# Sine attention with a mixture of experts on one core: the values of two units are summed together behind every fourth slot's scores

## Chip, core and metric

The kernel runs on one core of one Trainium2 chip. The metric is the device time of one execution in microseconds; the time before is 473.99, the median of three runs (473.74 to 475.28).

## What is computed

x has 8 rows of 512 tokens of 128 numbers. The reference, cut to what matters:

```python
# attention, 16 heads of 8, on the normalised x
logits = jnp.einsum('bhqd,bhkd->bhqk', Q, K) / scale
attn = jnp.sin(OMEGA_0 * logits)
out = jnp.einsum('bhqk,bhkd->bhqd', attn, V)
x = x + jnp.einsum('bsd,ed->bse', out, Wo) + bo
# experts, on the normalised x: one shared, eight routed of which each token takes two
out = shared                      # silu(x @ Wg.T) * (x @ Wu.T) @ Wd.T
for e in range(E_ROUTED):
    out = out + cw[..., e:e + 1] * _expert(x, Wg[e], Wu[e], Wd[e])
x = x + out
```

There is no softmax: a sine is taken of every score, and its products with V are summed over the keys.

## The kernel before, in words

Each engine has a program of its own, written out by hand over one common count of slots, `a`. A row of x has 32 slots (`SLOTS`); b is the row and s the slot in it. In slot s ScalarE takes one sine, of 128 keys x 512 queries x two heads (`sine`, line 888). Two slots make a unit: four heads and one tile of 128 keys, 16 units in a row (`UNITS`). Behind slot 256 (`TAIL`) there are no more sines, only the rest of the experts' tiles.

On TensorE, in every even slot s, stand the scores of slots s and s+1 (`scores`, line 638: two matmuls each, on 64 rows of the array each, that run together). They go to `score[0]` and `score[1]`, two banks of PSUM each; the scores of slot u wait until the sine of slot u-2 has read the same buffer (`sined`). Behind them stand the values of one earlier unit (`sum_values`, line 651: four heads of 32 columns side by side, each in fp32, eight matmul instructions in all), added into `o_ps` over the 16 units of a row. They read one of four buffers `attn` (`RING`); the sine of unit k waits until unit k-4 is summed (`summed`). The first unit of a row waits until `copy_o` (line 895 on ScalarE from row 3 on, line 1003 on VectorE in the rows before) has read `o_ps` of the row before, in slot 3.

Behind the values come, in this order: in odd slots from row 1 on, where the plan has a tile, `down` of an earlier tile (six matmuls, lines 778 to 780) and `gate_up` of a new one (twelve, lines 760 to 762); and the projections of the next row, the output projection, the transpose and the routing of the row before, each in a slot of its own (`S_Q` = 3: line 607; `S_K` = 8: line 614; `S_V` = 11: line 620; `S_OUT` = 6: line 664; `S_XT2` = 16: line 677; `S_ROUTE` = 19; `S_PREFIX` = 23). `gate_up` has one bank `g_ps` until slot 258, so it waits until `hid` of the tile before it (line 1220 on VectorE, behind ScalarE's silu, line 909) has read it; `down` comes six slots behind its tile.

ScalarE takes in every slot the sine, then the slot's silu, then the slot's copies (`copy_xt` line 869 in slot 2, `scale_q` 875 in slot 4, `scale_k` 881 in slot 9, `copy_o` in slot 3, `copy_x2` 899 in slot 17; in rows 0 to 2 VectorE has these copies). All waits are on semaphores, and an engine's instructions go in the order of its program.

The values of unit k stand in slot 2k + 4 (`LAG`); units 14 and 15 of a row stand in slots 0 and 2 of the next row (`LAST_SUMS`), those of the last row in slots 256 and 257 (`TAIL_SUMS`).

Of the kernel before, what the change touches and what calls it, by code (L numbers as in the profile page):

```python
# [16 lines left out]
ROWS, SEQ, DM = 8, 512, 128  # L17
# [41 lines left out]
SLOTS = 2 * GROUPS * TT  # L59
UNITS = SLOTS // 2  # L60
RING = 4
LAG = 4
LAST_SUMS = {0: 14, 2: 15}
TAIL = ROWS * SLOTS
TAIL_SUMS = {0: 14, 1: 15}

# [227 lines left out]
def sine_attention_moe_kernel(nc, x, wq, bq, wk, bk, wv, bv, wo, bo, wgu, wd, wr, rb, ident, out):  # L296
    with ExitStack() as ctx:
# [293 lines left out]
        def _(pe):  # L591
# [13 lines left out]
            def project_q(n, bank):  # L605
                pe.wait_ge(xt_ready, n + 1)
                pe.matmul(bank, wq_s[:, :], xn_t[:, :], start=True, stop=True).then_inc(q_done, 1)
# [16 lines left out]
            def scores(b, u):  # L624
                j, kt, h = u // 2 // TT, u // 2 % TT, u % 2
                if b == 0 and kt == 0:
                    pe.wait_ge(q_placed, 2 * j + h + 1)
                    pe.wait_ge(k_placed, 2 * j + h + 1)
                if b and u == 0:
                    pe.wait_ge(q_loaded, b * 64)  # L630
                    pe.wait_ge(k_loaded, b * 64)
                if b or u >= 2:
                    pe.wait_ge(sined, b * SLOTS + u - 1)
                elif u == 1:
                    pe.wait_ge(v_ready, 1)
                for i in range(2):
                    rows = slice(64 * i, 64 * i + 64)
                    mm = pe.matmul(score[h][:, i, :], keys[b % 2][rows, 2 * j + h, kt * P:(kt + 1) * P],  # L638
                                   queries[b % 2][rows, 2 * j + h, :], start=True, stop=True)
                mm.then_inc(scored, 1)  # L640

            def sum_values(b, k):
                j, kt = k // TT, k % TT
                pe.wait_ge(sined, b * SLOTS + 2 * k + 2)
                if k == 0:
                    pe.wait_ge(v_ready, b + 1)
                    if b:
                        pe.wait_ge(o_ready, b)
                for i in range(PER):
                    h = (j * PER + i) * 32  # L650
                    mm = pe.matmul(o_ps[32 * i:32 * i + 32, :], vals[b % 2][:, kt, h:h + 32], attn[k % RING][:, i, :],  # L651
                                   start=(k == 0), stop=(k == UNITS - 1))
                mm.then_inc(summed, 1)
# [57 lines left out]
            def look_up(g, first, end):  # L711

                pe.wait_ge(experts_ready, g + 1)
                _, found = nc.values_load_multi_w_load_instructions(
                    expert[g][0:1, first:end], engines=[mybir.EngineType.PE], min_val=0, max_val=(ROUTED - 1) * P,
                    skip_runtime_bounds_check_because="tile_experts clamps the table")
                for k, value in enumerate(found):
                    place_of[g, first + k] = value
# [18 lines left out]
            def gate_up(i):  # L737
                kind, row, t, e = TILES[i]
                if kind == SPARSE:
                    n = LOAD_OF[RANK[i]]  # L740
                    first = (RANK[i] - LOADS[n][0]) * P
                    pe.wait_ge(xt_loaded[n % XT], 16 * (n // XT + 1))
                    hi, lo = (xt[n % XT][:, half, first:first + P] for half in range(2))
                else:
                    pe.wait_ge(x2t_ready, row + 1)
                    hi, lo = (x2_t[row % TURNED][:, half * SEQ + t * P:half * SEQ + (t + 1) * P] for half in range(2))
                pe.wait_ge(w_split, 1 if kind == SHARED else EXP)

                if i >= GU_MAIN + BANKS - 1:
                    pe.wait_ge(hid_ready, i - BANKS + 1)  # L750
                elif i:
                    pe.wait_ge(hid_ready, min(i, GU_MAIN))
                bank = gu_bank(i)
                look_ahead(i, GU_PIECES)
                for c in range(2 * CH):
                    if c == 2:
                        look_ahead(i + 1, GU_PIECES)
                    here = bank[:, c * P:(c + 1) * P]
                    hi_part, lo_part = piece(i, w_hi[c]), piece(i, w_lo[c])
                    pe.matmul(here, hi_part, hi, start=True, stop=False)  # L760
                    pe.matmul(here, hi_part, lo, start=False, stop=False)  # L761
                    mm = pe.matmul(here, lo_part, hi, start=False, stop=True)  # L762
                mm.then_inc(gu_done, 1)

            def down(i):
                wait_lo(pe, i)
                if i >= D_MAIN + BANKS:
                    wait_read(pe, i - BANKS)
                elif i:
                    wait_read(pe, min(i, D_MAIN) - 1)  # L770
                here = d_bank(i)
                look_ahead(i, D_PIECES)
                for c in range(CH):
                    if c == 1:
                        look_ahead(i + 1, D_PIECES)
                    hi, lo = (half[i % HB][:, c * P:(c + 1) * P] for half in (hid_hi, hid_lo))
                    hi_part, lo_part = piece(i, w_hi[2 * CH + c]), piece(i, w_lo[2 * CH + c])
                    pe.matmul(here, hi, hi_part, start=(c == 0), stop=False)  # L778
                    pe.matmul(here, lo, hi_part, start=False, stop=False)  # L779
                    mm = pe.matmul(here, hi, lo_part, start=False, stop=(c == CH - 1))  # L780
                mm.then_inc(down_done, 1)
# [6 lines left out]
            def put_keys(pair, bank):  # L788
                put_heads(bank, put_k_hi, put_k_lo, pair, first_k)

            def put_queries(pair, bank):
                put_heads(bank, put_q_hi, put_q_lo, pair, first_q)
# [18 lines left out]
            for a in range(END + 1):  # L811
                b, s = divmod(a, SLOTS)
                tail = a - TAIL
                ahead = s - FIRST_SHIFT if b == 0 else s
                if b < ROWS:

                    if s % 2 == 0:
                        scores(b, s)
                        scores(b, s + 1)
                    if s % 2 == 0 and s >= LAG:  # L820
                        sum_values(b, (s - LAG) // 2)
                    if s in LAST_SUMS and b:
                        sum_values(b - 1, LAST_SUMS[s])
                elif tail in TAIL_SUMS:
                    sum_values(ROWS - 1, TAIL_SUMS[tail])
                for k in BATCH_AT.get(a, ()):
                    look_up(*BATCHES[k])
                if a in PLACE_AT:
                    pair = PLACE_AT[a]
                    pe.wait_ge(k_placed, pair)  # L830
                    put_keys(pair, g_ps[:, :])
                    pe.wait_ge(q_placed, pair)
                    put_queries(pair, d_ps[:, :])
                for i in D_AT.get(a, ()):
                    down(i)
                for i in GU_AT.get(a, ()):
                    gate_up(i)
                if b + 1 < ROWS:
                    if ahead == S_XT1:
                        xt1(b + 1)  # L840
                    if ahead == S_Q:
                        project_q(b + 1, r_ps[:, :])
                    if ahead == S_K:
                        project_k(b + 1, r_ps[:, :])
                    if ahead == S_V:
                        project_v(b + 1, r_ps[:, :])
                if 1 <= b < ROWS:
                    if s == S_OUT:
                        project_out(b - 1)
                    if s == S_XT2:  # L850
                        xt2(b - 1)
                    if s == S_ROUTE:
                        route(b - 1)
                    if s == S_PREFIX and b - 1 in GROUP_OF and ROUTE_GROUPS[GROUP_OF[b - 1]][-1] == b - 1:
                        ranks(GROUP_OF[b - 1])
                if tail == E_OUT:
                    project_out(ROWS - 1)
                if tail == E_XT2:
                    xt2(ROWS - 1)
                if tail == E_ROUTE:  # L860
                    route(ROWS - 1)
# [677 lines left out]
```

## Time and profile before

| | |
|---|---|
| median of three runs | 473.99 us |
| span of the profiled execution | 471.0 us |
| around the span (473.99 - 471.0) | 3.0 us |
| TensorE busy with matmuls | 421.8 us, 90% |
| ScalarE busy | 348.0 us, 74% |
| VectorE busy | 305.0 us, 65% |
| GpSimd busy | 239.5 us, 51% |
| all sines (line 888) | 256 of 1024 ns |
| all value matmuls (line 651) | 1024 instructions, 136.4 us busy |
| slots 0 to 255 | from 17.6 us to 367.9 us of the span |
| granted clock of TensorE | 1.00 up to 420 us of the span, 0.92 behind it |

The own time of the profiled execution is its span and what lies around it, 474.0 us if it is taken as the median of the runs. Busy time of matmuls is the union of their records; they overlap, so an interval between the starts of two of them says more than their length.

### The profile page before, as it was taken

The numbers are of one execution on the slowest core, as the hardware profiler recorded it, in microseconds if no ns is written. First come the engines' busy times: TensorE is split into PE (matmuls) and PEld (weight loads), VectorE is DVE, ScalarE is ACT, GpSimd is POOL, SyncE is SP. The second block draws the span as 40 slices with busy tenths as digits, with TensorE's granted clock in tenths as the row PEclk, the third lists the DMA queues.
The fourth block names the chain that finished last, engine by engine and source line by source line (L and its number), as shares of the span: only waits on it lengthen the run. The fifth ranks groups of instructions, "written<-read, shape, count | busy, mean of one in ns | idle before, by whom it ended". The sixth has DMA issues, their size and how long they took to land.

```text
span 471.0 us, 13125 instructions
## 1 busy us (share of the span) xinstructions
PE 421.8 (90%) x4648; PEld 225.2 (48%) x4648; DVE 305.0 (65%) x1058; ACT 348.0 (74%) x551; POOL 239.5 (51%) x322
## 2 busy tenths in 40 slices
PE   2899989999989999989999999889999989799872
PEld 1422233333423354444544545444544678789871
DVE  6877585644735355748674648684557578488994
ACT  1577978978888987868778886778788476676640
POOL 5351541300287141315865886227684787568851
PEclk9999999999999999999999999999999999999987
DMA  5037679727218514672264626862112256541220
GB/s 170 4 104 211 134 239 292 185 92 201 48 43 267 122 33 132 163 153 57 74 186 139 143 67 183 183 137 63 52 42 58 74 120 131 135 121 46 71 63 29
DMA packets 82479, 56.11 MB, mean 119 GB/s; under 512 B 29040, under 2 KB 76784, under 8 KB 82416
## 3 DMA queue, kind: packets, MB, share of 16 engines
q1 hardware_dynamic: 78112, 47.74, 38.9%
q0 software_dynamic: 3584, 7.35, 6.0%
q8 instruction: 38, 0.62, 0.6%
q10 hardware_dynamic: 720, 0.20, 0.2%
q14 instruction: 25, 0.20, 0.1%
HBM read 22.62 MB, written 27.13 MB: 106 GB/s over the span
## 4 chain that ended last, share of the span: by engine, by line
PE 57%; DVE 15%; issue 10%; ACT 7%; POOL 5%; DMA 4%; SPq 1%; ACTq 0%; DVEq 0%; POOLq 0%
PE o_ps L651 17%; PE score L638 9%; ACT attn L888 5%; PE g_ps L760 4%; PE g_ps L762 4%; PE g_ps L761 4%; PE d_ps L778 3%; DVE hid L1220 3%; DVE x_all L1263 2%; PE r_ps L664 2%; ACT gate L909 2%; DMA y_back<-in_wd 2%; POOL y_back L1455 2%; PE r_ps L614 2%; PE d_ps L780 2%
## 5 line engine op out<-in xcount | busy, mean ns | idle before, releaser
L888 ACT ACTIVATE attn<-score 128x1024 f32<-128x1024 f32 x256 | 248.2, 1024 | 26.7 <-PE score L638 26.2
L1436 POOL TENSOR_TENSOR hid_lo<-hid,hid_hi 128x256 f16<-128x256 f32 x108 | 75.9, 703 | 137.3 <-DVE hid_hi L1227 124.3
L651 PE MATMUL o_ps<-attn,vals 128*32 128x512 f32 x1024 | 136.4, 605 | 0.8 <-ACT o_t L895 0.5
L638 PE MATMUL score<-queries,keys 64*128 64x512 f16 x512 | 82.5, 383 | 9.5 <-ACT attn L888 8.0
L1220 DVE SCALAR_TENSOR_TENSOR hid<-g_ps,gate 128x256 f32<-128x256 f32 x102 | 43.2, 423 | 54.1 <-ACT gate L909 53.0
L909 ACT ACTIVATE gate<-g_ps 128x256 f32<-128x256 f32 x102 | 39.2, 384 | 45.4 <-PE g_ps L762 43.6
L778 PEld LDWEIGHTS d_ps<-w_hi,hid_hi 128*128 128x128 f16 x198 | 19.3, 97 | 59.6 <-issue 53.0
L760 PE MATMUL g_ps<-xt,w_hi 128*128 128x128 f16 x248 | 44.8, 220 | 1.1 <-DVE hid L1220 1.0
L761 PE MATMUL g_ps<-xt,w_hi 128*128 128x128 f16 x248 | 44.8, 220 | 0.0
L762 PE MATMUL g_ps<-xt,w_lo 128*128 128x128 f16 x248 | 44.7, 219 | 0.0
L778 PE MATMUL d_ps<-w_hi,hid_hi 128*128 (+1 forms) x198 | 39.1, 223 | 5.1 <-issue 2.8
L638 PEld LDWEIGHTS score<-queries,keys 64*128 64x128 f16 x512 | 18.0, 94 | 52.5 <-ACT attn L888 32.6
L651 PEld LDWEIGHTS o_ps<-attn,vals 128*32 128x32 f32 x1024 | 20.2, 108 | 47.7 <-issue 47.5
L780 PE MATMUL d_ps<-w_lo,hid_hi 128*128 (+1 forms) x198 | 38.5, 220 | 0.0
L779 PE MATMUL d_ps<-w_hi,hid_lo 128*128 (+1 forms) x198 | 38.5, 220 | 0.0
L914 ACT ACTIVATE hid_hi<-hid 128x256 f16<-128x256 f32 x70 | 28.9, 413 | 11.7 <-DVE hid L1220 11.4
L1421 POOL TENSOR_TENSOR rstd<-var_eps,minus_half 128x4 f32<-128x4 f32 x16 | 17.3, 1081 | 31.8 <-DVE var_eps L1016 15.9
L760 PE MATMUL g_ps<-x_t,w_hi 128*128 128x128 f16 x160 | 29.2, 221 | 0.0
L761 PE MATMUL g_ps<-x_t,w_hi 128*128 128x128 f16 x160 | 29.0, 220 | 0.0
L762 PE MATMUL g_ps<-x_t,w_lo 128*128 128x128 f16 x160 | 29.0, 220 | 0.0
L1241 DVE COPY y_sb<-d_ps 128x128 f32<-128x128 f32 x47 | 13.4, 286 | 23.4 <-PE d_ps L780 23.3
L1431 POOL TENSOR_SCALAR w_hi<-y_back 128x128 f16<-128x128 f32 x54 | 17.4, 351 | 21.6 <-DMA y_back<-in_wd 21.6
(220 smaller groups left out, 985.7 us busy)
## 6 DMA issues: line engine op xcount, KB each, us to landing
y_sorted<-y_sb SPq DMA_DIRECT2D x84, 64.0 KB
q_four<-q_parts SPq DMA_DIRECT2D x14, 256.0 KB
queries<-q_four SPq DMA_DIRECT2D x14, 256.0 KB
k_four<-k_minus SPq DMA_DIRECT2D x14, 256.0 KB
keys<-k_four SPq DMA_DIRECT2D x14, 256.0 KB
x_sorted<-zeros SPq DMA_DIRECT2D x2, 1472.0 KB, 8.5
queries<-q_three SPq DMA_DIRECT2D x14, 192.0 KB
keys<-k_three SPq DMA_DIRECT2D x14, 192.0 KB
```

The lines of the kernel that those rows point to most:

```text
L638: mm = pe.matmul(score[h][:, i, :], keys[b % 2][rows, 2 * j + h, kt * P:(kt + 1) * P], queries[b % 2][rows, 2 * j + h, :], start=True, sto ...
L651: mm = pe.matmul(o_ps[32 * i:32 * i + 32, :], vals[b % 2][:, kt, h:h + 32], attn[k % RING][:, i, :], start=(k == 0), stop=(k == UNITS - 1))
L760: pe.matmul(here, hi_part, hi, start=True, stop=False)
L761: pe.matmul(here, hi_part, lo, start=False, stop=False)
L762: mm = pe.matmul(here, lo_part, hi, start=False, stop=True)
L778: pe.matmul(here, hi, hi_part, start=(c == 0), stop=False)
L779: pe.matmul(here, lo, hi_part, start=False, stop=False)
L780: mm = pe.matmul(here, hi, lo_part, start=False, stop=(c == CH - 1))
L888: act.activation(attn[k % RING][:, 2 * (u % 2):2 * (u % 2) + 2, :], score[u % 2][:, :, :], ACT.Sin, scale=SIN_SCALE).then_inc(sined, 1)
L909: act.activation(gate[i % 2][:, :], gu_bank(i)[:, 0:HID], ACT.Silu, scale=UNSCALE).then_inc(gate_ready, 1)
L1220: dve.scalar_tensor_tensor(out=hid[i % HR][:, :], in0=gu_bank(i)[:, HID:2 * HID], scalar=UNSCALE * HSCALE, in1=gate[i % 2][:, :], op0=ALU. ...
L1436: pool.tensor_tensor(hid_lo[i % HB][:, :], hid[i % HR][:, :], hid_hi[i % HB][:, :], ALU.subtract).then_inc(lo_by_pool, 1)
```

## The change

TensorE's program alone is changed. Scores stay where they are. The values of two units now stand behind the scores of slots 4, 8, ..., 28 (`QUAD`): units s/2 - 2 and s/2 - 1 of the row. Behind those of slots 2, 6, ..., 30 stand no values. Units 14 and 15 stand both in slot 0 of the next row, or, for the last row, in slot 256. Unit k with an even number stays in its slot (unit 14 too), each odd one moves two slots ahead; of the last row unit 15 moves from slot 257 to slot 256. `sum_values` and its waits stay as they are.

```diff
 RING = 4
-LAG = 4
-LAST_SUMS = {0: 14, 2: 15}
+QUAD = 4
 TAIL = ROWS * SLOTS
-TAIL_SUMS = {0: 14, 1: 15}
...
                     if s % 2 == 0:
                         scores(b, s)
                         scores(b, s + 1)
-                    if s % 2 == 0 and s >= LAG:
-                        sum_values(b, (s - LAG) // 2)
-                    if s in LAST_SUMS and b:
-                        sum_values(b - 1, LAST_SUMS[s])
-                elif tail in TAIL_SUMS:
-                    sum_values(ROWS - 1, TAIL_SUMS[tail])
+                    if s % QUAD == 0 and s:
+                        sum_values(b, s // 2 - 2)
+                        sum_values(b, s // 2 - 1)
+                if s == 0 and 1 <= b <= ROWS:
+                    sum_values(b - 1, UNITS - 2)
+                    sum_values(b - 1, UNITS - 1)
```

## Rows read from the trace of the kernel before

**Rows 1.** The page's first part: busy us, share, instructions of each engine.

```profile
PE 421.8 (90%) x4648; PEld 225.2 (48%) x4648; DVE 305.0 (65%) x1058; ACT 348.0 (74%) x551; POOL 239.5 (51%) x322
```

**Rows 2.** Timeline (start us, us, what), TensorE and its weight loads, row 4 slot 28.

```profile
216.81 0.39 PE L638 MATMUL score<-queries,keys 64*128 64x512 f16 x2
217.04 0.38 PE L638 MATMUL score<-queries,keys 64*128 64x512 f16 x2
217.34 0.16 PEld L651 LDWEIGHTS o_ps<-attn,vals 128*32 128x32 f32 x8 [0.42 <-issue]
217.35 0.64 PE L651 MATMUL o_ps<-attn,vals 128*32 128x512 f32 x4
217.80 0.61 PE L651 MATMUL o_ps<-attn,vals 128*32 128x512 f32 x4
218.34 0.23 PE L778 MATMUL d_ps<-w_hi,hid_hi 128*128 x1
...
219.46 0.39 PE L638 MATMUL score<-queries,keys 64*128 64x512 f16 x1
```

**Rows 3.** Timeline of the same slots, ScalarE and VectorE.

```profile
216.91 0.38 ACT L909 ACTIVATE gate<-g_ps 128x256 f32<-128x256 f32 x1 [0.38 <-PE g_ps L762]
217.24 1.94 ACT L888 ACTIVATE attn<-score 128x1024 f32<-128x1024 f32 x2
...
217.33 0.43 DVE L1220 SCALAR_TENSOR_TENSOR hid<-g_ps,gate 128x256 f32<-128x256 f32 x1
```

**Rows 4.** Timeline of row 2, slots 4 to 6, TensorE and ScalarE.

```profile
97.95 0.61 PE L638 MATMUL score<-queries,keys 64*128 64x512 f16 x4
...
99.48 0.39 PE L638 MATMUL score<-queries,keys 64*128 64x512 f16 x2
100.37 0.39 PE L638 MATMUL score<-queries,keys 64*128 64x512 f16 x2 [0.50 <-ACT attn L888]
...
98.38 2.86 ACT L888 ACTIVATE attn<-score 128x1024 f32<-128x1024 f32 x3 [0.65 <-PE score L638]
```

**Rows 5.** Timeline of row 0, TensorE, slots 0 and 6 to 8.

```profile
18.34 0.39 PE L638 MATMUL score<-queries,keys 64*128 64x512 f16 x2 [0.31 <-DVE vals L1041]
18.66 0.39 PE L785 MATMUL g_ps<-x_t,x_pack 128*128 128x512 f16 x1
...
19.10 0.38 PE L785 MATMUL d_ps<-x_t,x_pack 128*128 128x512 f16 x1
...
25.20 0.61 PE L638 MATMUL score<-queries,keys 64*128 64x512 f16 x4
...
27.71 0.39 PE L638 MATMUL score<-queries,keys 64*128 64x512 f16 x2 [0.52 <-ACT attn L888]
```

**Rows 6.** Timeline, TensorE: scores of slot 4, row 0, and of slot 28, row 7.

```profile
22.61 0.61 PE L638 MATMUL score<-queries,keys 64*128 64x512 f16 x4
...
362.59 0.60 PE L638 MATMUL score<-queries,keys 64*128 64x512 f16 x4
```

**Rows 7.** Timeline of row 3, slots 2 and 3, TensorE and ScalarE.

```profile
133.87 0.60 PE L638 MATMUL score<-queries,keys 64*128 64x512 f16 x4
...
135.87 1.13 PE L607 MATMUL r_ps<-xn_t,wq_s 128*128 128x512 f32 x2 [0.40 <-ACT xn_t L869]
...
136.60 0.62 ACT L895 ACTIVATE o_t<-o_ps 128x512 f32<-128x512 f32 x1
```

**Rows 8.** Timeline of row 5, slots 10 and 11, TensorE and ScalarE.

```profile
239.70 0.61 PE L638 MATMUL score<-queries,keys 64*128 64x512 f16 x4
...
240.65 1.94 ACT L888 ACTIVATE attn<-score 128x1024 f32<-128x1024 f32 x2
```

**Rows 9.** Timeline of row 5, slots 18 to 20, TensorE.

```profile
252.07 0.61 PE L638 MATMUL score<-queries,keys 64*128 64x512 f16 x4
...
255.36 0.39 PE L638 MATMUL score<-queries,keys 64*128 64x512 f16 x2 [0.53 <-ACT attn L888]
```

## The prediction

> **What bounds the kernel now.** I read the busy shares first: TensorE has work for 90% of the span and ScalarE for 74%, so TensorE looks like the bound [rows 1]. A share says nothing of who waits for whom inside a slot, so I then laid one ordinary pair of slots out in time (slots 28 and 29 of row 4). TensorE starts the scores of the first slot at 216.81 and those of the second 0.23 us later; the values of one unit start 0.31 after that, in two waves 0.45 apart; the next matmul of another kind starts 0.54 after the second wave, so a unit costs 1.00. The tile's 18 matmuls and the gap behind them take 1.11, and the next pair starts at 219.46: 0.54 + 1.00 + 1.11 = 2.65 us, with no wait in it [rows 2]. ScalarE starts the two sines 0.43 and 1.35 after the pair's start and ends the second at 2.37, then idles 0.38 [rows 3]. Here TensorE is the bound, by 0.3 us or so.
>
> Where a pair has little beside scores and values it is the other way round. Behind slot 4 of row 2 the next pair starts after 1.53, but its second scores start only 2.42 after the pair's start, having waited 0.50 for a sine [rows 4]. That wait is the key: score[0] and score[1] are the only two places for scores, and the second scores of a pair need the second sine of the pair before, which cannot end before 2.37. In row 0 the same distance is once 2.51 (25.20 to 27.71) [rows 5]. So 2.42 is the least time from the start of a pair to the second scores of the next, however little TensorE has to do.
>
> **The change, part by part.** Call the pairs that start at slots 0, 4, 8 ... A and the others B; F is what a pair does behind its values up to the next pair's start. Two units go behind the scores of A, none behind those of B. All are computed, in the same order.
>
> *Waits of the moved units.* The second unit of A needs the sines of slots s-2 and s-1. The scores of slot s+1, in front of it on TensorE, already wait for the sine of s-1, so it adds no wait of its own. The sines' wait for a free attn buffer: unit k-4 is summed where it was, or two slots earlier. I cost both at nothing; the cover is that order of the code.
>
> *What A costs.* Between the second unit of A and the first there is no change of operand shape. The trace of before has no two units back to back. The nearest row is the 0.45 between the waves of one unit: 2 x 0.45 = 0.90 for the second unit. The ends are 0.88 (two back-to-back 512-column matmuls take 0.44 in slot 0, from 18.66 to 19.10, and a unit is four such passes [rows 5]) and 1.00 (nothing saved). I take 0.90. From the second scores of A to the start of B: 0.31 + 1.00 + 0.90 + F_A = 2.21 + F_A.
>
> The Trainium skill, TensorEngine Tiling, Key Properties, says that a change of tiling mode drains the engine; by that the second unit is spared one drain, as 0.54 against 0.45 says [rows 2], and nothing of the sum changes. Its TensorE: Matmul & The Clock Gate, The mechanism, says that weight loads overlap running matmuls only in other row groups. By that rule the second unit would save nothing, 1.00 each, and the sum below would end at 501.1. The trace speaks against it: all eight loads of a unit, which use all 128 rows, start within 0.16 us of 217.34, while the first wave runs from 217.35 on [rows 2].
>
> *What B costs.* F follows scores directly. Slot 0 of row 0 shows that: 0.32 from the second scores to the next matmul [rows 5], the same as ahead of values. So B by itself is 0.54 + F_B long, and the second scores of the next A come at 0.77 + F_B or at the floor of 2.42, whichever is later. In the ordinary pair 0.77 + 1.11 = 1.88: TensorE waits 0.54 that it didn't wait before. One ordinary A and B together: 2.21 + 1.11 + 2.42 = 5.74 against 5.30.
>
> *The sum.* I read the 124 pairs from slot 4 of row 0 on in the same way, from start of scores to start of scores. From the second scores of the first to those of slot 28 of row 7, each 0.23 behind the start of its pair, it is 339.98 us [rows 6], 62 times A and B. F_A sums to 60.13, F_B to 69.16. Work alone is 62 x 3.08 + 60.13 + 69.16 = 320.25, so 19.7 of the 340.0 are waits, about 12.5 of them second scores for a sine. After the change the A parts are 62 x 2.21 + 60.13 = 197.15. The B parts:
> - 39 B with F_B of 1.11 or less and nothing special: the floor, 39 x 2.42 = 94.4. (27 of the 62 have F_B of 1.06 to 1.11, ten less than 1, eight none; six of these are among the special ones; two of 1.49 stand in slot 18.)
> - 9 long ones (F_B 1.77 to 2.10, 17.60 in all: output projection, ranks, a wide projection of row 0): 9 x 0.77 + 17.60 = 24.5. Only these hide the missing values' time and keep the saving of 0.10.
> - 5 at slot 2 of rows 3 to 7. ScalarE copies xn_t between the two sines, TensorE starts the query projection at 2.00 behind the copy, and it is 1.05 long [rows 7]: second scores at 3.28. In rows 4 to 6 a silu (0.33) is ahead of the copy of o_t, which holds the values of slot 4 up by 0.15: 3.28 + 3 x 3.43. In row 7, without the copy of xn_t, o_t is ready 0.52 late: 2.94. Together 16.5.
> - 4 at slot 10 of rows 3 to 6, behind ScalarE's copy of kf: the sines start at 0.95, the second ends at 2.89 [rows 8]: 3 x 2.95, and 2.68 in row 3. Together 11.5.
> - 5 at slot 18 of rows 3 to 7, behind the copy of x_t: 252.07 to 255.36 is 3.30 [rows 9]: 4 x 3.30, and 3.02 in row 3. Together 16.2.
>
> The B parts are 163.2, the stretch 360.3, that is +20.3. To this come: the B tile's gate and up products need hid of the A tile, whose silu starts 0.10 behind the next pair's start and whose hid is ready at 0.95 [rows 3], while they are due at 0.87 in B (they were due at 1.87). With the time to be seen by TensorE I take 1.05; the floor hides that in short pairs (room up to 1.41), in six long ones it costs about 0.12 each: +0.7. The last A saves 0.1, and behind slot 256 units 14 and 15 stand together instead of on either side of a tile: 0.1. Sum: +20.8.
>
> The profiled execution spans 471.0, the median of the runs is 474.0, so 3.0 lie around the span. 471.0 + 20.8 = 491.8, and 494.8 as a time. The first two pairs, the tail behind slot 256 and the DMA queues keep their work; later rows give every load more time. SP, POOL and the order on VectorE and ScalarE aren't touched.
>
> **Rivals.**
> 1. *TensorE alone sets the pace.* Then each removed change of shape is a gain: 63 x 0.10 = 6.3, time 467.7. It is the other sign, and needs B pairs with F_B of 1.65 or more, or a second sine that ends by 1.83; of 62 B only 15 are so long, and the second sine ends at 2.37 or later in all pairs. A shared cover of all 62 isn't in the trace. Chance 0.04. The drain rule of TensorEngine Tiling named above would give this if nothing else were at work.
> 2. *The hid chain becomes the bound of B.* If VectorE has some 0.4 us queued ahead of hid (hid itself is 0.43 [rows 3]), gate and up of B start behind 1.41, and each further 0.1 costs in some 30 pairs. At 0.35 beyond: +10.5, time 505. Against it: VectorE has idle time in every A, which grows. Chance 0.12.
> 3. *A smaller loss.* Other waits of before lie inside F (a table load in slot 16 of rows 4 and 6, xn_t in slot 2) and are counted in full; with more time between they may go. At 6 us less: 489. Chance 0.12.
> 4. *It changes nothing that can be measured*, loss and saving cancelling: 474. It needs an F_B of 1.55 on average, where it is 1.12 (69.16 / 62). Chance 0.02.
>
> **How the numbers follow.** Forecast 0.70 at 494.8. Unknown prices move it: the second unit, -1.3 (0.88) to +6.3 (1.00); the floor at 2.51, +3.5. The range 487 to 505 holds these and reaches to rivals 2 and 3. About 0.3% is what a measurement of this kernel can tell from no change. Faster 0.05 (rival 1 and a little), same 0.02, slower 0.93.
>
> **What would show it.** In the changed kernel: 16 value matmuls within 1.9 + 0.1 us behind every fourth slot's scores; second scores of these slots starting 0.86 behind the first and waiting some 0.5 for a sine in nearly every A, and never in B with a long A ahead; TensorE's idle time ahead of scores, released by ScalarE, up by some 20 us; ordinary fours of 5.7 us. Fours of 5.2 all over would make rival 1 right; gate and up matmuls of B waiting for hid longer than 0.2, with the scores behind them late, rival 2. If the fours in row 0 are not longer than before, the floor is wrong.

## The result, and the profile of the changed kernel

The changed kernel takes 501.25 us (median of five runs, 495.83 to 502.66) where the kernel before takes 473.74 (five runs): a ratio of 1.0575, with an interval from 1.0533 to 1.0617. The profiled execution is the one of 495.83 us, with a span of 493.9 against 471.0. One execution of the twelve of `mixed`, a kernel further down, took 1362.31 us; it is in none of the ratios, and why it did isn't known. One line each of the first two parts of the changed kernel's page, and one group of its fifth:

```profile
PE 423.6 (86%) x4648; PEld 233.4 (47%) x4648; DVE 299.9 (61%) x1058; ACT 343.6 (70%) x551; POOL 240.1 (49%) x322
...
PEclk9999999999999999999999999999999989999996
...
L636 PE MATMUL score<-queries,keys 64*128 64x512 f16 x512 | 86.2, 383 | 25.4 <-ACT attn L886 23.8
```

Against [rows 1] the engines have done about the same work (TensorE 423.6 us for 421.8, ScalarE 343.6 for 348.0), and every share has fallen: what was added is idle time. The view of waits names it. Its lines say who waited for whom, how many us in total, how often, and the longest. Of the kernel before, TensorE:

```profile
PE score L638 <- ACT attn L888: 8.0, 16, 1.1
...
PE r_ps L700 <- DVE mask L1151: 1.7, 4, 0.6
...
PE g_ps L760 <- DVE hid L1220: 1.0, 1, 1.0
```

Of the changed kernel:

```profile
PE score L636 <- ACT attn L886: 23.8, 55, 1.0
...
PE r_ps L698 <- DVE mask L1149: 4.6, 4, 1.3
PE g_ps L758 <- DVE hid L1218: 3.3, 5, 1.2
```

Scores wait for a sine 55 times instead of 16. The timeline of row 4, slots 28 to 31, TensorE (start us, us, what), answers to [rows 2]:

```profile
232.96 0.39 PE L636 MATMUL score<-queries,keys 64*128 64x512 f16 x2
233.53 0.39 PE L636 MATMUL score<-queries,keys 64*128 64x512 f16 x2 [0.18 <-ACT attn L886]
233.85 1.92 PE L649 MATMUL o_ps<-attn,vals 128*32 128x512 f32 x16
235.71 0.23 PE L776 MATMUL d_ps<-w_hi,hid_hi 128*128 x1
...
236.82 0.60 PE L636 MATMUL score<-queries,keys 64*128 64x512 f16 x4
237.36 0.23 PE L776 MATMUL d_ps<-w_hi,hid_hi 128*128 x1
...
237.91 0.22 PE L758 MATMUL g_ps<-xt,w_hi 128*128 128x128 f16 x1
...
238.67 0.39 PE L636 MATMUL score<-queries,keys 64*128 64x512 f16 x2
```

Pair A starts at 232.96. Its second scores start 0.57 later, not 0.23. Its sixteen value matmuls run from 233.85, and the tile follows at 235.71: two units cost 1.86. Pair B starts at 236.82, with its tile 0.54 behind; the next A starts at 238.67. A is 3.86 long and B 1.85. An A and its B are called a four, after their four slots; this one takes 5.71 us, against 2 x 2.65 = 5.30 before. B's start to the next second scores is 1.85 + 0.57 = 2.42. Why they wait is on ScalarE in the same slots, which answers to [rows 3]:

```profile
236.92 0.38 ACT L907 ACTIVATE gate<-g_ps 128x256 f32<-128x256 f32 x1 [1.34 <-PE g_ps L760]
237.25 1.94 ACT L886 ACTIVATE attn<-score 128x1024 f32<-128x1024 f32 x2
```

The silu (line 907) and both sines keep ScalarE from 236.92 to 239.19, which is 2.37 behind B's start at 236.82, as in the kernel before. But ScalarE has idled 1.34 us ahead of them, where it idled 0.38. TensorE's long A keeps ScalarE without scores, and its short B then waits for the sines.

### The profile page after: what moved, and what is told of

Its sections match the earlier page's. It is cut to its first block, busy times and chain, and to the rows that moved or that the text cites. A ratio compares the mean times of both kernels' runs of the same rounds, so it can differ in the third digit from the quotient of the medians.

```text
span 493.9 us, 13125 instructions
## 1 busy us (share of the span) xinstructions
PE 423.6 (86%) x4648; PEld 233.4 (47%) x4648; DVE 299.9 (61%) x1058; ACT 343.6 (70%) x551; POOL 240.1 (49%) x322
## 4 chain that ended last, share of the span: by engine, by line
PE 55%; issue 13%; ACT 12%; DVE 11%; DMA 3%; POOL 3%; SPq 1%; ACTq 1%; DVEq 0%
PE o_ps L649 23%; ACT attn L886 10%; PE score L636 9%; PE g_ps L758 3%; PE g_ps L760 3%; PE g_ps L759 3%; DVE x_all L1261 2%; PE d_ps L776 2%; POOL y_back L1453 2%; PE r_ps L612 2%; DVE hid L1218 1%; DMA bq_s<-in_bq 1%; PE r_ps L618 1%; PE d_ps L778 1%; PE d_ps L777 1%
## 5 line engine op out<-in xcount | busy, mean ns | idle before, releaser
L649 PE MATMUL o_ps<-attn,vals 128*32 128x512 f32 x1024 | 123.1, 598 | 0.8 <-ACT o_t L893 0.5
L636 PE MATMUL score<-queries,keys 64*128 64x512 f16 x512 | 86.2, 383 | 25.4 <-ACT attn L886 23.8
L649 PEld LDWEIGHTS o_ps<-attn,vals 128*32 128x32 f32 x1024 | 27.0, 109 | 56.4 <-issue 55.0
L636 PEld LDWEIGHTS score<-queries,keys 64*128 64x128 f16 x512 | 19.0, 93 | 71.8 <-ACT attn L886 46.2
L912 ACT ACTIVATE hid_hi<-hid 128x256 f16<-128x256 f32 x70 | 28.9, 413 | 11.7 <-DVE hid L1218 11.4
L1429 POOL TENSOR_SCALAR w_hi<-y_back 128x128 f16<-128x128 f32 x54 | 17.0, 346 | 24.5 <-DMA y_back<-in_wd 24.5
```

## Experiments

The distance from the second scores of slot 4, row 0, to those of slot 28, row 7, is called the stretch, as in [rows 6]: 339.98 us before, 363.36 changed. Chips differ (the kernel before takes 489.9 us on one of them and 473.0 on another), so times are compared as ratios to the kernel before on the same chip. `a_again`, `a_tail`, `b_half` and `a_half` ran on one chip, the filled kernels and `mixed` on a second, the others on a third. The kernel before was profiled on none of these, so a stretch can be compared between kernels of one chip, and less surely with 339.98 and 363.36.

### Is the time of the changed kernel the time of its order of work, and does the last row matter?

`a_again` is the changed kernel on another chip.

> The changed kernel once more, for the spread of its time and for where TensorE's granted clock falls. Profiled at 495.8 with a mean clock of 0.988 it took 5 to 7 us less than its other four runs, which had 0.981 to 0.985. If the floor of the second scores is all of the loss, the stretch from row 0 slot 4 to row 7 slot 28 stays at 363 us in any profile, and what lies above 496 us sits in dips of the clock behind slot 256. If dips fall inside the rows, where TensorE now waits, the stretch itself grows with them.

Measured: 517.73 us, ratio 1.0553 (1.0511 to 1.0596). The loss repeats. The stretch doesn't stay at 363, as I had expected it to: it is 375.03. Three falls of TensorE's granted clock to half, 3.4 us each, lie in it, which is 5.1 us at most. And TensorE idles 1.87 and 1.14 us ahead of scores in row 3, where the profile names nothing that it waits for; the profiled run of the changed kernel has no such gap there. The kernel before is 16 us slower on this chip too, so the chip is the likely cause, but no profile of the kernel before on it shows that.

`a_tail` puts the last row's unit 15 back into slot 257:

```diff
-                    sum_values(b - 1, UNITS - 1)
+                    if b < ROWS:
+                        sum_values(b - 1, UNITS - 1)
+                if tail == 1:
+                    sum_values(ROWS - 1, UNITS - 1)
```

> The changed kernel, but the last row's unit 15 stands in slot 257 as before. Floor theory: within 0.3 us of the changed kernel, as nothing of its loss is behind slot 256. If the two units side by side in slot 256 move the clock's dips or the first tiles behind it, this one is back by several us (down to 495 at the median).

Measured: 520.82 us, ratio 1.0635 (1.0581 to 1.0688). It lies above `a_again` by 3 us, where at most 0.3 was expected, with intervals that overlap; the stretches of the two are 375.73 and 375.03. So nothing of the loss is won back by moving the last row's unit.

### Is it the sines' time? Half sines

`b_half` is the kernel before and `a_half` the changed one, with each sine over half the queries:

```diff
-                act.activation(attn[...][:, 2 * (u % 2):2 * (u % 2) + 2, :], score[u % 2][:, :, :], ACT.Sin,
+                act.activation(attn[...][:, 2 * (u % 2):2 * (u % 2) + 2, 0:SEQ // 2], score[u % 2][:, :, 0:SEQ // 2], ACT.Sin,
...
+            act.wait_ge(consts, 1)
             copy_xt(0)
...
+            for i in range(RING):
+                pool.memset(attn[i][:, :, :], 0.0)
```

The last lines fill `attn` with zeros on GpSimd before it does anything else. They take 7.05 us, and the first scores start at 23.06 us in `b_half` and 22.83 in `a_half`, where it was 17.64 and 17.22. So both have 5.4 to 5.6 us at the start that have nothing to do with the order of work; the difference of the two is free of it, the ratios to the kernel before aren't. The same holds for the two kernels without the silu, below.

> The kernel before, with each sine taken of half its queries only (the other half of the sines is left out and stands as zeros). Floor theory: the second scores can start some 1.6 us behind the pair's start instead of 2.42, so the 12.5 us of waits for a sine go: about 461 to 464 us. If ScalarE is never in the way (TensorE alone), it stays at 474.

> The changed kernel with the same half sines left out. Floor theory: B pairs of 1.65 to 1.85 us are longer than the floor of about 1.6 less 0.23, so the loss goes: per four slots 0.15 saved (the second unit costs 0.86, not 1.00), and in some 30 B pairs with a tile the 0.21 that gate and up wait for hid comes back uncovered: 9 saved, 6 lost, so 1 to 6 us below the half-sine kernel before. If the hid chain is the cause of the loss, it stays some 15 to 20 us above it; if the drain between shapes is all there is, 9 below.

Measured: `b_half` 487.84 us, ratio 0.9952 (0.9926 to 0.9979); `a_half` 499.47, ratio 1.0183 (1.0141 to 1.0225). Both expectations failed. `b_half` was to be 461 to 464 us on a chip where the kernel before takes 474, a ratio of at most 0.979; even without the 5.4 us at its start it would be about 0.985. TensorE's waits for a sine did go (0.2 us, from 8.0), but its stretch is 338.17, 1.8 us shorter than the one of the kernel before on the other chip: other waits took their place, one of 2.1 us at slot 8 of row 3 among them for which the profile names nothing. And `a_half`, which was to be below `b_half` by 1 to 6 us, is 11.6 us above it, its stretch 11.9 longer. With whole sines the changed order costs 27.8 us on this chip (517.73 against 489.9). So something over half of the loss went with the sines' time. The rest has another cause. TensorE's waits in `a_half`:

```profile
PE g_ps L758 <- DVE hid L1219: 8.2, 11, 1.4
PE score L636 <- ACT attn L886: 5.0, 8, 0.9
PE r_ps L698 <- DVE mask L1150: 4.6, 4, 1.3
```

and in `b_half`:

```profile
PE g_ps L760 <- DVE hid L1221: 1.8, 3, 1.2
PE r_ps L700 <- DVE mask L1152: 1.8, 4, 0.6
...
PE score L638 <- ACT attn L888: 0.2, 1, 0.2
```

With the sines out of the way, it is hid and mask from VectorE that the short B waits for. I formed a second theory: the 1.0 us of values behind B's scores covered not one chain but every chain that ends in B, through ScalarE and VectorE alike. The silu stands in the chain of hid, so I took it out too.

`b_half_ns` and `a_half_ns` leave the silu out as well:

```diff
-                for i in HID_AT.get(a, ()):
-                    silu(i)
...
-                dve.wait_ge(gate_ready, i + 1)
+                dve.wait_ge(gu_done, i + 1)
...
+            for i in range(2):
+                pool.memset(gate[i][:, :], 1.0)
...
```

> The kernel before with half of each sine and the silu left out: the base for the run beside it. It waits for hid 4 us in all with the silu, so it should be 2 to 5 us below the half-sine kernel before, which was 0.995 of the kernel before: 0.985 to 0.995.

> The half-sine changed kernel, with the silu left out as well: hid is taken from g_ps and a constant gate, so it is ready some 0.4 us sooner. Theory now: behind the floor of the second scores lies the wait of gate and up for hid, and either alone keeps TensorE waiting. With both taken away the removed changes of shape show: against the kernel before with the same left out, 9 us saved less 3 or so that the ranks still wait for their mask, 3 to 8 us less. Rival: if it is still 8 us or more above it, something else than the sine and hid (the other projections' chains, VectorE's queue) holds TensorE.

Measured: `b_half_ns` 478.02 us, ratio 0.9759 (0.9718 to 0.98), faster than I had expected; `a_half_ns` 483.88, ratio 0.9877 (0.9824 to 0.993). The changed order should have come out ahead here and is 5.9 us behind, its stretch 3.7 longer. The traces part by place. Where nothing is waited for, in 18 fours, the changed order does gain: 5.15 us against 5.29, the saved change of shape at last. That is 2.5 us in all, where I had counted on 9. In the fours that hold the ranks it loses 0.85 to 0.87 us in rows 2, 4, 6 and 7, 3.4 in all. In row 4 the pair at slot 22, which ends with the ranks, lasts 2.93 us in `b_half_ns` with a unit in it, and 2.93 in `a_half_ns` without. In row 7 fours lose 0.6 to 0.9 where `gate_up` waits for hid, the first seven of row 0 0.1 to 0.7, slot 0 of rows 3 and 5 and slot 28 of row 6 0.7 to 0.9. Two fours gain far more than 0.14, which keeps the sum at +3.7. At slot 16 of row 5 (1.23) a wait of 1.03 for `x_pack` is gone. At slot 8 of row 3 (2.07) the gain isn't the order's: in `b_half_ns` TensorE idles 1.96 us ahead of the key projection, for nothing that the profile names, and its granted clock is at half for the projection, which takes 2.02 us for 1.09:

```profile
147.44 2.02 PE L614 MATMUL r_ps<-xn_t,wk_s 128*128 128x512 f32 x2 [1.96 <-issue]
```

Without that one place the changed order would be some 2 us further behind. In TensorE's waits in `a_half_ns` the same names are left:

```profile
PE r_ps L698 <- DVE mask L1148: 4.0, 4, 1.1
PE g_ps L758 <- DVE hid L1217: 3.5, 5, 1.4
...
PE score L636 <- ACT attn L886: 3.1, 6, 0.6
```

### Does TensorE have time to spare in B, and none in A?

Six more matmuls of 128 columns into `o_ps`, with a zero operand, behind the values (or what stands there) of 49 pairs of rows 1 to 7: in the changed kernel in B (`a_fillB`) or in A (`a_fillA`), in the kernel before in B (`b_fillB`). B's slots have s % 4 == 2, A's 0:

```diff
+                if a == SLOTS:
+                    pe.wait_ge(zeroed, 1)
+                    pe.wait_ge(consts, 3)
+                if 1 <= b < ROWS and s >= 4 and s % 4 == 2:
+                    for _ in range(6):
+                        pe.matmul(o_ps[:, 0:P], id16[:, :], zeros[:, 0:P], start=False, stop=False, skip_group_check=True)
```

> The changed kernel with 49 times six extra matmuls (0.33 us, adding zeros to o_ps) behind the scores of slots 6, 10 ... 30 of rows 1 to 7, the B pairs, ahead of their tile. Floor theory: in 38 of the 49 the second scores behind it wait for the sine anyway, and 1.65 to 1.85 + 0.33 + 0.23 is no more than 2.42, so it costs only in the 11 long ones: +3 to +4 us. If TensorE's work is the bound, or the hid chain is: 49 x 0.33 = +16 (hid: +16 less what the waits for hid take in, some +9).

> The same 49 x 0.33 us of extra matmuls in the changed kernel, but behind the values of slots 4, 8 ... 28, the A pairs. Floor theory: A is on the path in full, +15 to +16.5 us over the changed kernel. Any theory in which both kinds of pair count alike gives the same for this and for the extra matmuls in B.

> The kernel before with the same extra matmuls behind the values of slots 6, 10 ... 30. Floor theory: in rows 4 to 7 TensorE is the bound and pays them in full (28 x 0.33 = 9.2), in rows 1 to 3 about half goes into waits for a sine: +11 to +15 us over the kernel before.

Measured, as ratio and stretch: `a_fillB` 1.0519 (1.0464 to 1.0574), 364.50, that is +1.1 on the changed kernel; `a_fillA` 1.084 (1.0783 to 1.0896), 378.43, +15.1; `b_fillB` 1.0257 (1.0204 to 1.0309), 351.36, +11.4 on the kernel before. The same matmuls cost 15 us in A, 11 in the kernel before, and nothing that the ratio shows in B, less even than the 3 to 4 us that I had expected. The timeline of `a_fillB`, TensorE, row 4, slots 26 and 28:

```profile
231.80 0.61 PE L636 MATMUL score<-queries,keys 64*128 64x512 f16 x4
232.33 0.51 PE L829 MATMUL o_ps<-zeros,id 128*128 128x128 f16 x6
...
233.78 0.83 PE L636 MATMUL score<-queries,keys 64*128 64x512 f16 x4
234.54 1.93 PE L649 MATMUL o_ps<-attn,vals 128*32 128x512 f32 x16
```

B is 1.98 long instead of 1.85, and the second scores of the next A take up the rest: their wait shrinks from 0.34 to 0.21. The values start at 234.54, 2.74 behind B's start, where they started 2.73 behind it in the changed kernel (0.31 + 2.42). Work put into B goes into the wait.

### Two units together only where the wait is there already

`mixed` is the kernel before with ten pairs of units put together, in pairs A whose B is held by something else than its own work (slot 4 of rows 2 to 7, slot 8 of rows 0 and 4 to 6; in slots 6 and 10 behind them the value matmuls are gone):

```diff
+PAIRED = {(0, 8), (2, 4), (3, 4), (7, 4)} | {(b, s) for b in (4, 5, 6) for s in (4, 8)}
...
-                    if s % 2 == 0 and s >= LAG:
+                    if s % 2 == 0 and s >= LAG and (b, s - 2) not in PAIRED:
                         sum_values(b, (s - LAG) // 2)
+                    if (b, s) in PAIRED:
+                        sum_values(b, (s - LAG) // 2 + 1)
```

> The kernel before with two units together only where the changed kernel's trace gained: slot 4 of rows 2 to 7, slot 8 of rows 0 and 4 to 6, that is where the pair behind is long or where the longer values cover a wait. Floor theory, from the fours of both traces: 0.1 + 0.2 + 0.8 + 3 x (0.3 + 0.4) + 0.1 = 3.4 us below the kernel before, about 470.4. If two units together cost by themselves (the clock, the hid chain), 474 or more.

Measured: 470.55 us, ratio 0.9944 (0.9916 to 0.9972), stretch 336.67 (-3.3). As expected. It is faster than both kernels, by little, but the interval leaves out 1. TensorE's waits for a sine stay at 7.1 us in 16 places, where they were 8.0 in 16 before: a sine is not what these fours wait for in the end, so the saved changes of shape are kept.

### Waiting scores let pass a unit

`a_late` is the changed kernel with the first of the two units between the two scores of A, so that TensorE has work while it would wait:

```diff
                         scores(b, s)
+                        if s % QUAD == 0 and s:
+                            sum_values(b, s // 2 - 2)
+                        if s == 0 and b:
+                            sum_values(b - 1, UNITS - 2)
                         scores(b, s + 1)
                     if s % QUAD == 0 and s:
-                        sum_values(b, s // 2 - 2)
                         sum_values(b, s // 2 - 1)
...
```

> The changed kernel, but with the first of its two units between the scores of slots s and s+1, where TensorE now waits for the sine. Floor theory: the second scores start at 1.31 behind the first instead of waiting to 0.57 to 0.91 idle, at the price of one more change of shape: an ordinary four 5.58 instead of 5.71, one without a tile 0.4 to 0.5 less. In all 8 to 10 us less than the changed kernel, so 1.035 to 1.042 of the kernel before. If TensorE's own work is what counts, it is 63 x 0.14 = 9 us slower than the changed kernel.

Measured: 510.05 us, ratio 1.0419 (1.0377 to 1.0461), at the slow end of what I had expected. The ordinary four is 5.60 us instead of 5.71; where A's scores had not waited, A got 0.25 longer (3.75 for 3.50). Waits for a sine fall to 9.4 us in 13 places, but hid now takes their part:

```profile
PE score L636 <- ACT attn L890: 9.4, 13, 1.0
...
PE g_ps L758 <- DVE hid L1222: 8.4, 12, 1.2
```

`best` has the kernel before as its base, puts units together in seven of the pairs of `mixed`, and puts the one unit between the scores in nine pairs whose second scores waited:

```diff
+PAIRED = {(7, 4)} | {(b, s) for b in (4, 5, 6) for s in (4, 8)}
+BETWEEN = {(0, 8), (0, 16), (1, 6), (2, 6), (3, 6), (3, 20), (5, 20), (7, 20), (6, 22)}
...
                         scores(b, s)
+                        if (b, s) in BETWEEN:
+                            sum_values(b, (s - LAG) // 2)
                         scores(b, s + 1)
-                    if s % 2 == 0 and s >= LAG:
+                    if s % 2 == 0 and s >= LAG and (b, s - 2) not in PAIRED and (b, s) not in BETWEEN:
                         sum_values(b, (s - LAG) // 2)
+                    if (b, s) in PAIRED:
+                        sum_values(b, (s - LAG) // 2 + 1)
```

> The kernel before with two edits, each only where its trace calls for it: the values between the two scores in the nine pairs in which the second scores waited 0.6 to 1.2 us and work stands behind them (slots 8 and 16 of row 0, 6 of rows 1 to 3, 20 of rows 3, 5, 7, 22 of row 6), and two units together at slot 4 of rows 4 to 7 and slot 8 of rows 4 to 6. Floor theory: 2.2 us from the paired units, about 0.5 to 0.6 from each pair with values between the scores (1.1 in row 3, 0.9 in row 6): 6.2. Together 8.4 less: 465.6 where the kernel before takes 474, a ratio of 0.982. If the waits only move on, 0.994 or more.

Measured: 485.66 us where the kernel before takes 490.13, ratio 0.9918 (0.9889 to 0.9946): half of the gain expected. It is the lowest ratio of all the kernels with the whole computation, but its interval overlaps that of `mixed`. Row 0 gains as said (slots 8 and 16, 0.59 us each), so do slots 4 to 7 of rows 1 to 3 (0.26, 0.57 and 1.00 us). The fours at slot 20 fall short of the 0.5 to 0.6 expected: in row 3 it gains 0.37, in rows 5 and 7 it loses 0.13 and 0.11. Its timeline in row 5, TensorE:

```profile
253.45 0.39 PE L640 MATMUL score<-queries,keys 64*128 64x512 f16 x2
253.77 1.07 PE L653 MATMUL o_ps<-attn,vals 128*32 128x512 f32 x8
254.77 0.39 PE L640 MATMUL score<-queries,keys 64*128 64x512 f16 x2
...
256.20 0.39 PE L640 MATMUL score<-queries,keys 64*128 64x512 f16 x2
257.14 0.39 PE L640 MATMUL score<-queries,keys 64*128 64x512 f16 x2 [0.55 <-ACT attn L894]
```

The second scores start 1.32 behind the first. Waiting for their sine, they start 0.92 behind it (0.39 of scores and a wait of 0.53, [rows 9]). So the sine behind them starts 0.4 late, and the next pair's second scores, at 257.14, wait 0.55 for it. Where the next pair is short, values put between the two scores only hand the wait on. At slot 8 of row 3 the profile also has 1.53 us of idle time of TensorE for which it names nothing; whether the kernel before has it on this chip isn't known, so how much of the missing gain is the order's stays open.

## Why the prediction was right, and where its terms were off

**The bound.** Right. The distance of 2.42 from the start of a pair to the second scores of the next is found to the hundredth in the ordinary fours, and as 2.51 in row 0. Behind ScalarE's copies it is 3.28 in slot 2 (3.28 predicted, [rows 7]), 3.03 in slot 10 (2.95, [rows 8]), 3.29 in slot 18 (3.30, [rows 9]). The TensorE-only rival gave 5.2 for the fours; they are 5.71, and 5.74 was predicted. The filled kernels show that it is a floor and no sum of work. The sign that I had named for it was off: in the ordinary B the second scores start 0.57 behind the first, not 0.86, because B is 0.21 longer (see Hid below), and the waits for a sine grew by 15.8 us, not by 20. The floor is the same; less of it is a wait.

**The second unit.** It costs 0.86 (1.86 for both), not 0.90: 62 x 1.86 = 115.3 where the sum had 117.8, -2.5 us. It is below both my ends (0.88 and 1.00). The four waves start 0.45, 0.43 and 0.43 apart, and the next shape starts 0.54 or 0.55 behind the last: only the last wave pays for the change. The Trainium skill, TensorE: Matmul & The Clock Gate, The mechanism, says that weight loads overlap running matmuls only in other row groups; from that I had worked out 1.00 for the second unit, and the trace, with 0.86, disagrees.

**The values of slot 4.** `copy_o` holds them 0.18 longer in rows 4 to 6 and 0.54 in row 7, where 0.15 and 0.52 were foreseen. The sum had counted this under B's slot 2, and it lies in A: the five pairs at slot 2 took 15.6 instead of 16.5, and A's waits +1.1. The two cancel, to 0.2 us.

**The A parts** are 196.3 (197.15 predicted), **the B parts** 167.1 (163.2). The stretch is +23.4 instead of +20.3.

**The mis-sized term: nine long B.** I took 24.5 us and they take 28.7. Four of them, at slot 22 of rows 2, 4, 6 and 7, end with the ranks, and cost 14.6 where I had 10.4. The other five take 14.1, as I had it. The step was "9 x 0.77 + F_B": I had F_B, 1.81 and more, as if it were work of TensorE. But it begins when the values end and it ends behind the ranks, which start when VectorE's mask is there. The timeline of the kernel before, TensorE, row 4, slot 22:

```profile
208.18 0.61 PE L638 MATMUL score<-queries,keys 64*128 64x512 f16 x4
208.71 1.07 PE L651 MATMUL o_ps<-attn,vals 128*32 128x512 f32 x8
...
211.20 0.21 PE L700 MATMUL r_ps<-mask,upper 128*128 128x72 f16 x1 [0.31 <-DVE mask L1151]
```

VectorE in the same slots:

```profile
208.70 0.42 DVE L1220 SCALAR_TENSOR_TENSOR hid<-g_ps,gate 128x256 f32<-128x256 f32 x1 [0.79 <-ACT gate L909]
...
210.96 0.18 DVE L1151 TENSOR_SCALAR mask<-rest 128x32 f16<-128x32 f32 x1
```

The changed kernel, TensorE, at the same place:

```profile
224.26 0.60 PE L636 MATMUL score<-queries,keys 64*128 64x512 f16 x4
224.79 0.23 PE L776 MATMUL d_ps<-w_hi,hid_hi 128*128 x1
...
227.28 0.21 PE L698 MATMUL r_ps<-mask,upper 128*128 128x72 f16 x1 [1.10 <-DVE mask L1149]
```

and VectorE:

```profile
224.78 0.42 DVE L1218 SCALAR_TENSOR_TENSOR hid<-g_ps,gate 128x256 f32<-128x256 f32 x1 [0.79 <-ACT gate L907]
...
227.04 0.18 DVE L1149 TENSOR_SCALAR mask<-rest 128x32 f16<-128x32 f32 x1
```

The ranks start 3.02 behind the pair's start in both, VectorE starts on the mask 2.78 behind it in both: hid starts 0.52 behind, and 2.26 us of VectorE's program lie from there to the mask. That chain, and not TensorE's work, sets the pair's length; with a unit in it TensorE waited 0.31 there, without it 1.10. Such a wait stood in the kernel before's trace at all four places (1.7 us in all, in the view of waits above), and it was the sign that F_B had a floor of its own. It is a floor like that of the sines, from another engine, and I had looked for it in one chain only.

**Hid.** The 0.21 that B's `gate_up` waits (1.85 long instead of 1.65) was foreseen as 0.18, and the floor hides it, as said. The +0.7 that I had added for the long ones doesn't show: the four at slot 6 take 2.86 to the next second scores, which is 0.77 and their F_B of 2.09 with nothing added, and at slot 22 the wait for the mask stands behind it.

**The sum** for the profiled execution: stretch +3.1 against the forecast (second unit -2.5, A's waits and the rounding of 0.314 to 0.31 in 62 pairs +1.6, long B +4.2, other B -0.3). The span is 493.9 where I had 491.8: outside the stretch I had +0.5 (hid +0.7, the end -0.2), and it is -0.5. Its time is 495.8 where I had 494.8, because 1.9 us and not 3.0 lie around the span. That the profiled execution came within 1 us is in part luck, since the errors have both signs. The median is 6.5 above the forecast, and the change of the medians is 27.5 us where I had 20.8.

**The rest, which stays open.** The other four runs are at 501.0 to 502.7, 5 to 7 us above the profiled one, on the same chip. Their mean granted clocks are 0.981 to 0.985, its own 0.988. None of them was profiled. In the profile of `a_again`, with a mean of 0.981, TensorE's clock falls to its lower level for 3.4 us at four places ahead of the end, two of them in row 3; in the profiled run of the changed kernel there is one such place. Two more falls would take 7 us at half clock, 3.4 us at most of lost time. They fit a half of the difference; the other half isn't explained, and no record shows which of these runs had falls, or where. That the median of a kernel's runs would be its profiled execution's time, as I had taken it for the kernel before, was a step of my prediction that did not hold.

**The rivals.** TensorE alone (467.7): out, by the fours. The hid chain (505): the floor covers it with whole sines, and it shows as soon as the sines are short (`a_half`) or let pass (`a_late`). It wasn't the bound, but it is the next one. The smaller loss: out; inside F waits did go (slots 4 to 7 of row 3 are 1.0 us shorter), but the ranks alone took 4.2.

## What to carry to other kernels

Before work is taken out of a slot of an in-order engine, list every chain through other engines that ends in that slot, with its time from the slot's start (here the second sine 2.37, hid 0.95, the mask 2.96 and the ranks behind it 3.02): the slot can't get shorter than the latest, and the work that was taken away is added in full where it went. An interval in the trace that ends at a wait, even a small one, isn't work, and can't be counted as such when what stands ahead of it is moved. Putting matmuls of one shape together pays where the slot that loses them has work of its own behind them (`mixed`: 0.6% faster).

## What the runs showed of the hardware

Two units of values back to back cost 1.86 us, not twice 1.00; a change of shape from 128x32 to 128x128 costs 0.09 to 0.12 (0.54 or 0.55 from the last wave to the next shape, 0.43 to 0.45 between waves), and is paid only by the last wave ahead of it.

TensorE's granted clock falls in the middle of the program, behind a stretch in which TensorE has done little. Windows of the changed kernel, behind slot 256 (window, length, then busy us and instructions of TensorE, its weight loads, VectorE, ScalarE and GpSimd, granted clock, DMA share, GB/s):

```profile
393.40:396.80 3.40, 1.52 (x25) 1.23 (x23) 2.04 (x8) 1.26 (x3) 1.65 (x2) 1.00 0.29 77
396.80:400.20 3.40, 3.40 (x32) 3.40 (x32) 0.42 (x1) 0.78 (x3) 2.62 (x3) 0.50 0.22 57
```

and of `a_again`, row 3:

```profile
164.80:168.20 3.40, 1.74 (x16) 0.43 (x16) 0.19 (x1) 2.76 (x4) 2.79 (x3) 1.00 0.62 219
168.20:171.60 3.40, 3.40 (x23) 1.09 (x16) 0.00 (x0) 1.01 (x2) 0.15 (x1) 0.50 0.21 53
```

The granted clock is 1.00 (2.4 GHz) and then 0.50 (1.2 GHz); in the rows ahead of the falls TensorE was busy for 1.52 and 1.74 us of 3.40. The kernel before has one such fall ahead of its end too, at 452.3 us. How many there are differs between two executions of the changed kernel on two chips (one and four). That an order of work which leaves TensorE idle makes its time less certain isn't shown: the five runs of the changed kernel span 6.8 us and those of the kernel before 2.4, but 17 runs of the kernel before on another chip span 6.7.
